# Attention scores of a 192-step macaron pipeline in two bursts, with the second half of W1's products between them

## Chip, cores and metric

One core of one Trainium2 chip. The metric is the device time of the kernel in microseconds, median of the runs.

## The reference, cut to what matters

```python
def _L0_ffn_ref(x, ...):              # called twice, with _L0_attn_ref between
    for i in range(6):
        x = attn_layer(shift_tokens(x), Wqkv[i], q_scale[i], k_scale[i], Wo[i]) + x
        x = ffn_layer(shift_tokens(x), ln_g[i], ln_b[i], W1[i], b1[i], W2[i], b2[i]) + x
    return x
# attn_layer: 16 heads of 64, q and k normalised and rotated, then in windows of 32
#   each with the window before it:
sim = einsum('bhwie,bhwje->bhwij', q, look(k)) * 8.0   # masked, softmax over 64 keys
out = einsum('bhwij,bhwje->bhwie', softmax(sim), look(v))
# ffn_layer: layer norm, then
hg = xn @ W1 + b1; a, gate = split(hg, 2)
return a * gelu(gate) @ W2 + b2       # W1 is 128 x 682, W2 is 341 x 128

x = x + 0.5 * _L0_ffn_ref(_layernorm(x), ...)
x = x + _L0_attn_ref(_layernorm(x), ...)      # a linear recurrence over time
x = x + 0.5 * _L0_ffn_ref(_layernorm(x), ...)
```

The input is 2 x 1024 tokens of 128 channels in float32.

## The kernel before, in words

The 2048 tokens are 16 tiles of 128, and the two passes through six layers are 12 layers, so there are 192 tiles of work (`T`). The kernel is a software pipeline written out by hand: in step `s` every engine works on several tiles at once, each at another lag behind `s`: the token shift and transpose at lag 0 (`L_X`), the projections of q and k at lag 1 (`L_QKV`), `values` (projection of v), the transposes of q and k, and the scores at lag 2 (`L_S`), the softmax at 3 (`L_SM`), attention times values and Wo at 4 (`L_AV`, `L_WO`), the first half of the feed-forward layer at 5 (`L_F`), its second half at 6 (`L_F2`). All 198 steps are unrolled into one long program for each engine; there are no loops left on the chip. Each engine runs its own list in order, and semaphores that count steps tie the lists together (`k.wait(sem, lag)`).

TensorE's list in a step (`step` in the tensor block): the projections `project(1)`, `project(0)` (line 484), eight transposes of q (line 495), `attend` (line 539), `project(2)`, `project(3)`, eight transposes of k (line 495), Wo (line 594), eight transposes of the probabilities (line 602), the transpose of the normed tile (line 607), W2 (line 622), `values(1)` and `values(0)` (line 490), the transpose of the next tile (line 639), `hidden(1)` and `hidden(0)`, that is the gate half and the other half of W1's products (line 503), and last `scores`.

`hidden(k, a)` writes three products of 128x114 weights into `proj[:, a, :]`, each as two passes in float32. `proj` is a PSUM tile of two banks that q, k, v and W1's products share, so `hidden(k, a)` waits for `a_v[a]`, ScalarE's copy of the v tile out of the same bank (line 677). ScalarE's gelu (line 740) reads the bank of `hidden(1)` and needs another activation table than the exponential; VectorE's `hT` (line 1001) multiplies gelu's result with the bank of `hidden(0)`, and waits for `p_f[0]` and `a_gelu`.

`scores` first writes a mask into the two banks of `sps` (line 519, one product of 128x512 in bfloat16 for each) and then adds, for each of 8 head pairs, 2 bank halves, 2 window groups and 2 heads, a small product of 64x32 weights (line 527): 64 products, each in two passes, each with its own weight load. The last one signals `p_S`, for which VectorE's maximum (line 1008) waits; ScalarE's copies into `qT` and `kT` wait for it a step later. Bank 0 of `sps` also holds the scratch values of VectorE's reciprocal root, so the scores wait for `v_rs` (its last step is `rn`, line 848), for `v_sub` (VectorE's subtraction that has read the last scores), for `a_qT`, `a_kT`, and in even steps for `a_car`. After it the next step begins with `project(1)`, which waits for `a_xT` (ScalarE's last write of `xsT`, line 750) and `a_gelu`; `project(0)` waits for `v_h` (VectorE's `hT`).

Of the kernel before, what the change touches and what calls it, by code (L numbers as in the profile page):

```python
# [25 lines left out]
PAIRS = HEADS // 2  # L26
# [20 lines left out]
L_X, L_QKV, L_S, L_SM, L_AV, L_WO, L_F, L_F2 = 0, 1, 2, 3, 4, 4, 5, 6  # L47
# [10 lines left out]
def macaron(nc, x_in, w_in, w_out, b_out, w_qkv, q_scale, k_scale, w_o,  # L58
            w_1, w_2, b_2, c_cols, c_rope, c_mask, c_ident, out):
    with ExitStack() as ctx:  # L60
# [3 lines left out]
        def sem(name):  # L64
            return ctx.enter_context(nc.semaphore(name))
# [86 lines left out]
        p_xT, p_qT, p_kT, p_S, p_pT = sem("p_xT"), sem("p_qT"), sem("p_kT"), sem("p_S"), sem("p_pT")  # L152
# [6 lines left out]
        a_v = [sem(f"a_v{c}") for c in range(2)]  # L159
# [308 lines left out]
        def _(pe):  # L468
# [29 lines left out]
            def hidden(k, a):  # L498

                at = (k.ffn if k.reg is not None else (k.s - L_F) // TILES % DEPTH) * 2 * FH  # L500
                for c in range(3):
                    rows = min(FC, FH - c * FC)
                    last = mm(proj[0:rows, a, c * P:(c + 1) * P],  # L503
                              w1[:, at + a * FH + c * FC:at + a * FH + c * FC + rows],
                              xnT[:, :], start=True, stop=True, skip_group_check=True)
                last.then_inc(p_f[a], 1)
# [4 lines left out]
                    mm(ops[:, 1, 0:3 * P], hT[:, 0, :], hT[:, :, :].rearrange("p c n -> p (c n)"), start=True, stop=True,  # L511
                       skip_group_check=True)

            def scores(k):
                first = k.off("first", L_S, lambda u: ((POS - 1 - u % POS) // (POS - 1)) * 512)
                par = k.parity(L_S)
                for ty in range(2):
                    m = mask[:, bass.ds(first, 512)] if ty == 0 else mask[:, 0:512]
                    mm(sps[:, ty, :], idb[:, :], m, start=True, stop=False, skip_group_check=True)
                for p in range(PAIRS):  # L520
                    for ty in range(2):
                        for g in range(2):
                            for hp in range(2):
                                w = 2 * ty + g
                                at, rows = par * P + w * WIN, slice(hp * DH, (hp + 1) * DH)
                                to = (2 * g + (hp ^ ty)) * WIN
                                last = mm(sps[to:to + WIN, ty, p * 64:(p + 1) * 64], qT[rows, p, w * WIN:(w + 1) * WIN],  # L527
                                          kT[rows, p, at:at + 2 * WIN], start=False, stop=True, skip_group_check=True)
                last.then_inc(p_S, 1)

            def attend(k):
                par = k.parity(L_AV)
# [11 lines left out]
            def step(k):  # L544
# [44 lines left out]
                if k.on(L_WO):  # L589
# [3 lines left out]
                    for p in range(PAIRS):  # L593
                        last = mm(ops[:, 0, 0:P], oT[:, p, :], wo[:, bass.ds(w + p * P, P)], start=(p == 0),  # L594
                                  stop=(p == PAIRS - 1))
                    last.then_inc(p_wo, 1)
                if k.on(L_SM):
# [3 lines left out]
                    for p in range(PAIRS):  # L601
                        last = tr(tps[:, p, :], prob[:, p, :, :].rearrange("p a b -> p (a b)"), idf[:, :])  # L602
# [5 lines left out]
                if k.on(L_F2):  # L608
# [12 lines left out]
                    for c in range(3):  # L621
                        last = mm(ops[:, 1, 3 * P:4 * P], hT[0:FC, c, :], w2[0:FC, bass.ds(at + c * P, P)],
                                  start=(c == 0), stop=(c == 2))
# [16 lines left out]
                if k.on(L_F):  # L640
                    k.wait(a_xnT, L_F)
                    if k.s == L_F:
                        pe.wait_ge(d_mlp, 16 * len(mlp_consts))
                    for a in (1, 0):
                        k.wait(a_v[a], L_S)
                        hidden(k, a)
                if k.on(L_S):

                    k.wait(v_sub, L_S + 1)
                    k.wait(v_rs, L_QKV, per=RS_STEPS)  # L650
                    k.wait(a_qT, L_S)
                    k.wait(a_kT, L_S)
                    if k.parity(L_S) == 0:
                        k.wait_even(a_car, L_S)
                    if k.reg is None and k.s == L_S:
                        pe.wait_ge(s_idb, 1)
                        pe.wait_ge(s_mask, 1)
                    scores(k)

            pe.wait_ge(c_zero2, 1)  # L660
            idle(WARM)
            pe.wait_ge(d_id, 16)
            pe.wait_ge(c_zero, 1)
            pipeline(pe, step)

# [563 lines left out]
```

## Time and profile before

| | us |
|---|---|
| median of 3 runs | 3307.64 (3303.78 to 3307.83) |
| the profiled execution's own time | 3302.78 |
| its span, first to last instruction | 3301.0 |
| PE busy | 3177.7 (96%) |
| PE weight loads busy | 2377.1 (72%) |
| DVE busy | 2994.8 (91%) |
| ACT busy | 2543.2 (77%) |
| POOL busy | 2229.6 (68%) |

PE is TensorE's matmuls and PEld its weight loads, which overlap them; DVE is VectorE, ACT ScalarE, POOL GpSimd. Durations of matmuls overlap, since they are pipelined: the distance from one start to the next tells what one costs. In a timeline each row is a run of equal instructions with its start, its length to the end of the last, and its count; in brackets stands how long the engine was idle before it and what ended that. "issue" is idle time for which the profile shows no wait. L503 is line 503 of the kernel.

### The profile page before, as it was taken

How to read it: one execution, taken by the hardware profiler on the slowest of the kernel's cores; microseconds unless marked ns; L12 is line 12 of the kernel's file. 1: busy time of each engine (PE TensorE's matmuls, PEld its weight loads, DVE VectorE, ACT ScalarE, POOL GpSimd, SP SyncE). 2: the span in 40 equal slices, each digit the busy share in tenths (PEclk: the TensorE clock that was granted, in tenths of full speed). 3: DMA queues.
4: the chain of work that ended last, by engine and by line, in shares of the span. 5: the costliest groups of instructions: out<-in, count | busy, mean ns of one | idle time of the engine just before them, and what ended most of it. 6: DMA issues, size and time to landing. Idle time of an engine off the chain costs nothing. (4 is left out here: it accounts for less than half of the span.)

```text
span 3301.0 us, 125954 instructions
## 1 busy us (share of the span) xinstructions
PE 3177.7 (96%) x50984; PEld 2377.1 (72%) x51176; DVE 2994.8 (91%) x7143; ACT 2543.2 (77%) x4144; POOL 2229.6 (68%) x1454
## 2 busy tenths in 40 slices
PE   7999999999999999999889999999999999999998
PEld 3777777777777777776667777777777777777776
DVE  7999999999899999999999998899999999999995
ACT  3877878777787777777667777788777777887775
POOL 6666666666666666667777766666666666666663
PEclk9999999999999999999999999999999999999999
DMA  4111111111111111111111111111111111111111
GB/s 124 44 48 44 48 45 48 45 48 44 47 45 48 45 48 45 47 44 39 37 37 47 45 48 45 40 48 46 45 44 48 45 48 45 48 45 48 47 52 38
DMA packets 134996, 155.84 MB, mean 47 GB/s; under 512 B 75539, under 2 KB 108439, under 8 KB 134423
## 3 DMA queue, kind: packets, MB, share of 16 engines
q1 hardware_dynamic: 129815, 144.42, 15.9%
q8 instruction: 413, 6.77, 0.9%
q10 hardware_dynamic: 4608, 3.34, 0.4%
q14 instruction: 160, 1.31, 0.1%
HBM read 33.38 MB, written 1.05 MB: 10 GB/s over the span
## 5 line engine op out<-in xcount | busy, mean ns | idle before, releaser
L1084 POOL TENSOR_TENSOR rot<-rot,swp 128x1024 f32<-128x1024 f32 x384 | 907.2, 2363 | 132.5 <-DVE rot L867 132.5
L484 PE MATMUL proj<-wq,xsT 128*128 128x512 f32 x1536 | 773.4, 622 | 55.9 <-DVE hT L1001 22.4
L673 ACT ACTIVATE sq<-proj 128x512 f32<-128x512 f32 x768 | 437.6, 596 | 400.6 <-PE proj L484 387.3
L1093 POOL TENSOR_TENSOR rot<-rot,rn 128x1024 f32<-128x1024 f32 x384 | 724.6, 1910 | 0.0
L1074 POOL TENSOR_TENSOR rt<-rt,half 128x1 f32<-128x1 f32 x192 | 105.8, 551 | 743.1 <-DVE rt L937 743.1
L861 DVE TENSOR_TENSOR swp<-proj,tab 128x512 f32<-128x512 f32 x768 | 522.0, 680 | 9.4 <-ACT sq L673 5.1
L867 DVE TENSOR_TENSOR rot<-proj,tab 128x512 f32<-128x512 f32 x768 | 518.9, 676 | 1.7 <-PE tps L495 1.6
L495 PEld LDWEIGHTS tps<-idf,rot 128*128 128x128 f32 x3072 | 362.6, 141 | 207.1 <-issue 205.1
L1078 POOL TENSOR_TENSOR prob<-prob,rr 128x1024 f32<-128x1024 f32 x192 | 365.8, 1905 | 174.7 <-DVE rr L949 174.7
L484 PEld LDWEIGHTS proj<-wq,xsT 128*128 128x128 f32 x1536 | 257.5, 189 | 293.0 <-issue 138.1
L495 PE MATMUL tps<-idf,rot 128*128 128x128 f32 x3072 | 402.0, 274 | 3.5 <-POOL rot L1093 1.9
L594 PE MATMUL ops<-wo,oT 128*128 128x128 f32 x3072 | 376.3, 276 | 4.0 <-ACT oT L695 4.0
L539 PE MATMUL ops<-pT,vb 128*64 128x64 f32 x6144 | 379.3, 225 | 0.0
L490 PE MATMUL proj<-wq,xsT 128*128 128x512 f32 x768 | 369.5, 601 | 3.5 <-DVE rot L867 3.3
L539 PE MATMUL ops<-pT,va 128*64 128x64 f32 x6144 | 369.6, 222 | 0.0
L594 PEld LDWEIGHTS ops<-wo,oT 128*128 128x128 f32 x3072 | 359.8, 193 | 4.3 <-issue 4.2
L527 PEld LDWEIGHTS sps<-kT,qT 64*32 64x32 f32 x24576 | 258.4, 105 | 121.5 <-issue 121.1
L722 ACT COPY pT<-tps 64x1024 f32<-64x1024 f32 x192 | 193.2, 1006 | 187.3 <-PE tps L602 187.3
L1001 DVE SCALAR_TENSOR_TENSOR hT<-proj,cols,fg 114x128 f32<-114x128 f32 (+1 forms) x576 | 166.8, 345 | 187.4 <-issue 179.1
L539 PEld LDWEIGHTS ops<-pT,vb 128*64 128x64 f32 x6144 | 311.6, 138 | 32.9 <-issue 32.6
L527 PE MATMUL sps<-kT,qT 64*32 64x64 f32 x24576 | 296.2, 225 | 33.3 <-issue 33.2
L503 PEld LDWEIGHTS proj<-xnT,w 128*114 128x114 f32 (+1 forms) x2304 | 273.5, 178 | 73.7 <-issue 67.9
(104 smaller groups left out, 6164.6 us busy)
## 6 DMA issues: line engine op xcount, KB each, us to landing
vb<-va SPq DMA_DIRECT2D x192, 384.0 KB, 3.5
vb<-va SPq DMA_DIRECT2D x192, 128.0 KB, 3.6
wq<-in_L_ffn_Wqkv SPq DMA_DIRECT2D x95, 192.0 KB, 3.4
xs<-Z SPq DMA_DIRECT2D x192, 32.0 KB
wo<-in_L_ffn_Wo SPq DMA_DIRECT2D x94, 64.0 KB, 2.8
xs<-Z SPq DMA_DIRECT2D x192, 28.0 KB
xs<-Z SPq DMA_DIRECT2D x192, 3.8 KB
xs<-Z SPq DMA_DIRECT2D x192, 0.2 KB
```

The lines of the kernel that those rows point to most:

```text
L484: mm(proj[:, c % 2, :], xsT[:, k.parity(L_QKV), 0:P], wq2[:, bass.ds(w + c * 512, 512)], start=True, stop=True).then_inc(p_qkv[c], 1)
L490: mm(proj[:, c, :], xsT[:, k.parity(L_S), 0:P], wq2[:, bass.ds(w + (4 + c) * 512, 512)], start=True, stop=True).then_inc(p_v[c], 1)
L495: last = tr(tps[:, p, :], rot[:, g * INNER + p * P:g * INNER + (p + 1) * P], idf[:, :])
L527: last = mm(sps[to:to + WIN, ty, p * 64:(p + 1) * 64], qT[rows, p, w * WIN:(w + 1) * WIN], kT[rows, p, at:at + 2 * WIN], start=False, stop ...
L539: last = mm(o4[hp * DH:(hp + 1) * DH, :, g, :], v, pT[:, 2 * p + g, hp, :, :].rearrange("p t i -> p (t i)"), start=True, stop=True, skip_g ...
L594: last = mm(ops[:, 0, 0:P], oT[:, p, :], wo[:, bass.ds(w + p * P, P)], start=(p == 0), stop=(p == PAIRS - 1))
L673: fn(sq[:, c * 512:(c + 1) * 512], proj[:, c % 2, :], ACT.Square).then_inc(a_sq[c], 1)
L861: v.tensor_tensor(halves(swp[:, c * 512:(c + 1) * 512]), swapped, tab[:, bass.ds(po + (2 * g + 1) * POS * DH, DH)] .rearrange("p (a d) -> ...
L867: v.tensor_tensor(heads(rot[:, c * 512:(c + 1) * 512]), heads(src), tab[:, bass.ds(po + 2 * g * POS * DH, DH)].unsqueeze(1) .to_broadcast( ...
L1078: g_.tensor_tensor(pr, pr, rr[:, :].unsqueeze(2).to_broadcast([P, HEADS, 2 * WIN]), ALU.mult).then_inc(g_nrm, 1)
L1084: g_.tensor_tensor(r, r, swp[:, g * INNER:(g + 1) * INNER], ALU.add).then_inc(g_add[g], 1)
L1093: g_.tensor_tensor(r, r, rn[:, g * HEADS:(g + 1) * HEADS].unsqueeze(2) .to_broadcast([P, HEADS, DH]), ALU.mult).then_inc(g_nm[g], 1)
```

## The change

The scores of a step are issued in two bursts of four head pairs instead of one burst of eight, and `hidden(0)` stands between them instead of ahead of the masks. The masks, with the waits of the scores, follow `hidden(1)`. `p_S` is signalled by the last product of the second burst.

```diff
--- before.py
+++ after.py
@@ -511,13 +511,15 @@
                     mm(ops[:, 1, 0:3 * P], hT[:, 0, :], hT[:, :, :].rearrange("p c n -> p (c n)"), start=True, stop=True,
                        skip_group_check=True)
 
-            def scores(k):
+            def masks(k):
                 first = k.off("first", L_S, lambda u: ((POS - 1 - u % POS) // (POS - 1)) * 512)
-                par = k.parity(L_S)
                 for ty in range(2):
                     m = mask[:, bass.ds(first, 512)] if ty == 0 else mask[:, 0:512]
                     mm(sps[:, ty, :], idb[:, :], m, start=True, stop=False, skip_group_check=True)
-                for p in range(PAIRS):
+
+            def scores(k, pairs):
+                par = k.parity(L_S)
+                for p in pairs:
                     for ty in range(2):
                         for g in range(2):
                             for hp in range(2):
@@ -526,7 +528,7 @@
                                 to = (2 * g + (hp ^ ty)) * WIN
                                 last = mm(sps[to:to + WIN, ty, p * 64:(p + 1) * 64], qT[rows, p, w * WIN:(w + 1) * WIN],
                                           kT[rows, p, at:at + 2 * WIN], start=False, stop=True, skip_group_check=True)
-                last.then_inc(p_S, 1)
+                return last
 
             def attend(k):
                 par = k.parity(L_AV)
@@ -641,9 +643,8 @@
                     k.wait(a_xnT, L_F)
                     if k.s == L_F:
                         pe.wait_ge(d_mlp, 16 * len(mlp_consts))
-                    for a in (1, 0):
-                        k.wait(a_v[a], L_S)
-                        hidden(k, a)
+                    k.wait(a_v[1], L_S)
+                    hidden(k, 1)
                 if k.on(L_S):
 
                     k.wait(v_sub, L_S + 1)
@@ -655,7 +656,13 @@
                     if k.reg is None and k.s == L_S:
                         pe.wait_ge(s_idb, 1)
                         pe.wait_ge(s_mask, 1)
-                    scores(k)
+                    masks(k)
+                    scores(k, range(PAIRS // 2))
+                if k.on(L_F):
+                    k.wait(a_v[0], L_S)
+                    hidden(k, 0)
+                if k.on(L_S):
+                    scores(k, range(PAIRS // 2, PAIRS)).then_inc(p_S, 1)
 
             pe.wait_ge(c_zero2, 1)
             idle(WARM)
```

## Rows read from the trace of the kernel before

**Rows 1.** The page: span, and busy time of each engine, share, instructions.
```profile
span 3301.0 us, 125954 instructions
...
PE 3177.7 (96%) x50984; PEld 2377.1 (72%) x51176; DVE 2994.8 (91%) x7143; ACT 2543.2 (77%) x4144; POOL 2229.6 (68%) x1454
```

**Rows 2.** The view of cores: span and mean granted TensorE clock.
```profile
core 0: 3301.0 us, clock 0.994
```

**Rows 3.** Timeline of PE: mask products of five following steps (start, us, engine, line).
```profile
293.65 0.38 PE L519 MATMUL sps<-mask,idb 128*128 128x512 bf16 x1
...
310.09 0.38 PE L519 MATMUL sps<-mask,idb 128*128 128x512 bf16 x1
...
327.41 0.38 PE L519 MATMUL sps<-mask,idb 128*128 128x512 bf16 x1
...
343.85 0.38 PE L519 MATMUL sps<-mask,idb 128*128 128x512 bf16 x1
...
360.21 0.38 PE L519 MATMUL sps<-mask,idb 128*128 128x512 bf16 x1
```

**Rows 4.** Timeline of PE, 824.05 to 828.5 us: the end of one step.
```profile
824.08 1.64 PE L503 MATMUL proj<-xnT,w 128*114 128x128 f32 x12
825.77 0.38 PE L519 MATMUL sps<-mask,idb 128*128 128x512 bf16 x1
826.08 1.48 PE L527 MATMUL sps<-kT,qT 64*32 64x64 f32 x128
827.68 1.10 PE L484 MATMUL proj<-wq,xsT 128*128 128x512 f32 x2
```

**Rows 5.** Line 527, the score passes: ns of one, least, median, most.
```profile
L527 PE MATMUL sps<-kT,qT x24576: 212/216/241, 40.1 to 3267.2; 64*32 64x64 f32 x200
```

**Rows 6.** Timeline of PE, 427.5 to 430 us: behind a late burst.
```profile
428.38 0.33 PE L527 MATMUL sps<-kT,qT 64*32 64x64 f32 x12 [0.87 <-issue]
428.66 1.54 PE L484 MATMUL proj<-wq,xsT 128*128 128x512 f32 x3
```

**Rows 7.** Timelines of ACT and of DVE, 824 to 829 us, same step.
```profile
824.17 0.59 ACT L677 COPY va<-proj 128x512 f32<-128x512 f32 x1 [0.23 <-PE proj L490]
824.78 1.28 ACT L740 ACT_TABLE_LOAD   x1
826.07 0.89 ACT L740 ACTIVATE fg<-proj,cols 114x128 f32<-114x128 f32 x3
...
827.38 0.20 ACT L750 ACTIVATE xsT<-xsT 64x1 f32<-64x1 f32 x1
...
824.56 0.19 DVE L848 SCALAR_TENSOR_TENSOR rn<-rt,sps 128x32 f32<-128x32 f32 x1
...
827.41 0.87 DVE L1001 SCALAR_TENSOR_TENSOR hT<-proj,cols,fg 114x128 f32<-114x128 f32 x3 [1.40 <-issue]
828.19 1.21 DVE L1008 TENSOR_REDUCE mx<-sps 128x16 f32<-128x1024 f32 x1
```

**Rows 8.** Timeline: `values` in the same step, its load and its four passes.
```profile
823.01 0.30 PEld L490 LDWEIGHTS proj<-wq,xsT 128*128 128x128 f32 x2 [0.60 <-DVE rot L867]
...
822.21 1.92 PE L490 MATMUL proj<-wq,xsT 128*128 128x512 f32 x4
```

**Rows 9.** Timeline of PEld: three bursts that stop; idle before in brackets.
```profile
310.40 1.24 PEld L527 LDWEIGHTS sps<-kT,qT 64*32 64x32 f32 x118 [0.42 <-issue]
312.69 0.17 PEld L527 LDWEIGHTS sps<-kT,qT 64*32 64x32 f32 x10 [1.06 <-issue]
...
426.13 1.22 PEld L527 LDWEIGHTS sps<-kT,qT 64*32 64x32 f32 x116 [0.42 <-issue]
428.38 0.17 PEld L527 LDWEIGHTS sps<-kT,qT 64*32 64x32 f32 x12 [1.03 <-issue]
...
194.02 1.24 PEld L527 LDWEIGHTS sps<-kT,qT 64*32 64x32 f32 x119 [0.42 <-issue]
196.86 0.16 PEld L527 LDWEIGHTS sps<-kT,qT 64*32 64x32 f32 x9 [1.60 <-issue]
```

**Rows 10.** The page, part 3: packets, MB, share of 16 DMA engines.
```profile
q8 instruction: 413, 6.77, 0.9%
```

**Rows 11.** Waits view: us in total, times, longest.
```profile
PEld sps L527 <- issue: 121.1, 232, 1.7
```

**Rows 12.** Windows view, line 527's loads from the burst's start: us, busy (x).
```profile
826.08:826.69 0.61, 0.61 (x67) 1.00 0.03 0
826.08:827.37 1.29, 1.29 (x128) 1.00 0.01 0
```

**Rows 13.** Timeline of PE: into and out of `attend`, and four passes unhindered.
```profile
813.10 1.04 PE L495 MATMUL tps<-idf,rot 128*128 128x128 f32 x8
814.07 0.28 PE L539 MATMUL ops<-pT,vb 128*64 128x64 f32 x2
...
815.86 0.29 PE L539 MATMUL ops<-pT,va 128*64 128x64 f32 x4
816.08 1.98 PE L484 MATMUL proj<-wq,xsT 128*128 128x512 f32 x4
...
805.89 1.88 PE L490 MATMUL proj<-wq,xsT 128*128 128x512 f32 x4
```

**Rows 14.** Timeline of PEld about the middle, 1620 to 1640 us.
```profile
1632.49 0.30 PEld L484 LDWEIGHTS proj<-wq,xsT 128*128 128x128 f32 x2 [2.34 <-DVE hT L1001]
```

## Prediction

> **What bounds the kernel now.** I read the busy shares first, then the timeline of the end of one step, then the waits of TensorE's weight loads, because the change only reorders TensorE's program. TensorE is busy 96% of the span, VectorE 91% [rows 1], and the granted clock is full nearly throughout [rows 2], so the clock has no part in this. The kernel is 192 pipelined steps, and the mask products of following steps start 16.44, 17.32, 16.44 and 16.36 us apart [rows 3]. Two questions follow: what sets the 16.4, and what makes one step 0.9 longer.
>
> What sets 16.4: at the end of a step (window 824 to 829) TensorE runs W1's twelve passes (`hidden`), the masks and the burst of 128 score passes, then the next step's first projection [rows 4]. The last score pass starts at 826.08 + 1.48 - 0.22 = 827.34 [rows 4, 5], the projection at 827.68, that is 0.34 later. After a burst that ended late for another reason the same hand-over took 428.66 - (428.38 + 0.33 - 0.22) = 0.17 [rows 6]. So TensorE waits some 0.15 here, and for this: ScalarE copies the value tile out at 824.17, loads the gelu table, runs gelu and writes `xsT` until 827.38 + 0.20 = 827.58 [rows 7], and the projection's weight load starts at 827.65. The end of a step is bound by ScalarE's chain behind `values`, with TensorE 0.15 behind it. VectorE stands close too: `hT` starts after gelu, `mx` starts when `hT` is done [rows 7], and VectorE's last rotation releases the load for `values` at 823.01 [rows 8].
>
> What makes a step long: in the step of 310.40 the burst's loads run to number 118, stop for 1.06 us with nothing to wait for, and end with ten more; at 426.13 they stop after 116 for 1.03, at 194.02 after 119 for 1.60 [rows 9]. The three are 116 us, or seven steps, apart. Instructions come to TensorE over a queue of 413 packets [rows 10]; 102,160 matmuls and loads [rows 1] are 247 to a packet (with the semaphore instructions a little more) and 532 to a step. So each step uses two packets and some 0.15 of a third, and a packet's end moves through the step and is back after seven. It hurts only late in the burst, where 256 instructions are used up in 1.3 us: the next packet is usable 2.29, 2.25 and 2.84 us after the burst began [rows 9]. The waits view has 232 idle stretches before these loads, 121.1 us in all [rows 11]; 192 are the ordinary 0.42 ahead of each burst (81 us), which leaves 40 of 1.01 us. One such stall of 1.06 made its step 0.92 longer [rows 3], the rest went into the 0.15 above. Now lost: 40 x (1.01 - 0.14) = 35 us.
>
> The Trainium skill, page "Advanced Engine Details and Errata", section ISA Cache, says that an instruction cache line is 16 KB or 256 instructions and that there are two; the trace agrees in the 247 and in the seven steps.
>
> **The change, part by part.** Nothing is added or removed: the six passes of the second half of W1 with their six loads, and the wait for `a_v[0]`, move from ahead of the masks to the middle of the burst. TensorE issues no DMA. What TensorE's order costs in an ordinary step:
> - Two bursts for one. Of the present one 67 loads are under way by 0.61 us, and all 128 take 1.29 [rows 12]: the front goes faster than the rest. Two of 0.61: -0.05.
> - Into the small tiles once more. The present kernel does that ahead of `attend`: eight transposes from 813.10, beat (1.04 - 0.27) / 7 = 0.11, so that the next would start at 813.98; it starts at 814.07 [rows 13]. +0.09.
> - Out of them once more. `attend`'s last four start at 815.86 and run 0.29, so the last starts at about 815.93; the projection starts 0.15 later and its four passes take 1.98 where they take 1.88 with the load hidden [rows 13]. With the ordinary beat of 0.02 taken off: +0.24.
> - `hidden(0)` no longer waits for the copy of `va`. Its six and `hidden(1)`'s six passes take 1.64 [rows 4] where twelve at the beat of 0.11 take 11 x 0.11 + 0.27 = 1.47; half of the difference is `hidden(1)`'s own wait, which stays. -0.08.
> - The masks come up 0.75 sooner and meet their wait for `v_rs`: VectorE's `rn` ends at 824.56 + 0.19 = 824.75 [rows 7], `hidden(1)` at about 824.80. Nothing, or a mask load that isn't prefetched, 0.10. Taken: +0.05. Queued behind that wait are only the masks and scores.
> - Slack taken up: -0.15 at the projection (above), -0.04 at `values`, whose four passes take 1.92 against 1.88 [rows 8, 13] because VectorE releases them late.
>
> Sum +0.06 us. Bounds: 0 (the switches cost half, as the queue is full behind the moved passes) to +0.20 (no slack used and an unhidden mask load). The switches are the largest term: the Trainium skill, page "TensorEngine Tiling (Array Packing)", Key Properties, says that changing the tiling mode drains the engine, which speaks against the change; the trace shows it as the 0.09 and 0.24 above.
>
> Who waits for the moved work: VectorE's `hT` needs `hidden(0)`. That would now be issued 0.31 + 0.61 + 0.8 after the first mask, last pass near 826.8, seen near 827.1; gelu ends at 826.96 and `hT` mostly starts right after. It costs VectorE 0 to 0.1, inside the bounds. The scores are complete about 0.25 later than now; `mx` has that to spare while `hT` runs (0.87). ScalarE's gelu needs `hidden(1)` alone, which doesn't move. This counts in some 170 steps; for 20 about the middle (1460 to 1800 us) VectorE is the bound: TensorE's load waits 2.34 us for `hT` there [rows 14]. 170 x 0.06 = +10 us.
>
> **The stalls.** A packet that ends in the second burst now takes in `hidden(0)`: from the first score pass to the last is 0.61 + 0.24 + 0.65 + 0.09 + 0.61 = 2.2 us, against 1.27. If the next packet is usable 2.27 us after the burst's begin as now, hardly a stall is left. But no row shows when it is asked for. TensorE's instructions ahead of the present burst are held last by the wait for `a_v[0]`, 1.27 us before the burst; afterwards by the wait for `v_rs`, 0.6 before it. An order placed as soon as that wait is over comes 0.65 later, and the stall is then 2.27 + 0.65 - 2.2 = 0.7. Taken: 0.65, since two of the three stalls end 2.29 and 2.25 us after the burst's begin. It strikes when the packet's end falls on the last 34 of the 256 places (the second burst's last 30 and the projection's first 4; a place further ahead has `hidden(1)` in its packet and time enough): 192 x 34/256 = 25 steps, 16 us. Bounds: 3 us left to 30 us left. Saved: 35 - 16 = 19 us (5 to 32).
>
> **Sum.** +10 - 19 = -9 us. The profiled execution took 3302.78 us, 3301.0 of it span, so 3294 for it; it stands 4.9 below the median of 3307.64, which gives 3299.
>
> **The rivals.**
> - *The stalls go almost wholly.* The order for the packet moves with the burst, 2.2 us suffice: saved 32, cost 10 or less, -22 to -35, so 3273 to 3286. For it: 2.25 and 2.29 are nearly 2.2. Against: 2.84 at 194 us, and the later wait. 0.22.
> - *The switches win: slower.* Place: the hand-overs score, W1, score in each ordinary step. Price: 0.33 for both, and if ScalarE's `xsT` or VectorE moves along with TensorE's delay (through `hidden(0)` to `hT` to the projection's `v_h`), the 0.19 of slack isn't there: +0.17 to +0.2 a step, 30 us, less 19: +11, 3319. It decides from +0.11 a step on (170 x 0.11 = 19). For it: `hT` and `mx` sit right behind each other. Against: 0.15 of idle at the projection in most steps. 0.20.
> - *The stalls only change place.* An order 0.65 later and a slower transfer leave 1 us each time on 25 to 30 steps; saved 8, cost 10: 3309, no change. 0.16.
> - My forecast: 0.42, its own range 3292 to 3306.
>
> That the change doesn't do what it says I leave out: the diff has every product once and the same waits.
>
> **How the numbers follow.** About 0.2% (6.6 us) is what a measurement of this kernel can tell from no change; the forecast of -9 lies just past it, so of its 0.42 I give 0.27 to faster and 0.15 to the same. Faster 0.27 + 0.22 = 0.49, same 0.15 + 0.16 = 0.31, slower 0.20. The range takes in the stall-free rival and the slower one: 3276 to 3324, about a tenth beyond either end.
>
> **What would show it.** Idle stretches before score loads of near 1 us: from 40 to some 25 of 0.65, all near the end of the second burst or at the projection behind it. The ordinary step from 16.40 to about 16.46. The projection's load no longer 0.24 late behind `xsT`. `hT` at most 0.1 later against gelu. The forecast is wrong if the ordinary step is 16.52 or more (then slower), or if stalls at scores are gone (then 3280). In the middle 20 steps nothing should move.

## The result, and the profile after

| | before | after |
|---|---|---|
| median of 5 runs each | 3307.64 us (3300.16 to 3307.96) | 3319.07 us (3316.81 to 3320.97) |
| span of the profiled execution | 3301.0 | 3316.7 |
| ordinary step (mean of two neighbours) | 16.40 | 16.52 |

The ratio is 1.0041, with a 95% interval of 1.0028 to 1.0053: the change makes the kernel slower by 0.4%. The page, the view of cores and two rows of the waits view after:

```profile
span 3316.7 us, 126146 instructions
...
PE 3229.7 (97%) x51176; PEld 2389.1 (72%) x51176; DVE 2997.6 (90%) x7143; ACT 2543.1 (77%) x4144; POOL 2229.9 (67%) x1454
...
q8 instruction: 413, 6.77, 0.8%
```
```profile
core 0: 3316.7 us, clock 0.995
```
```profile
PEld sps L529 <- issue: 115.1, 237, 1.7
PEld proj L484 <- DVE hT L1008: 37.0, 23, 2.9
```

VectorE, ScalarE, GpSimd, the clock and the instruction packets stand as before [rows 1, 2, 10]. PE's busy time is 52 us up, but that is mostly no work: before, the first of the two mask products has no record in any step [rows 3, x1], and now it has (x2, 0.59 us where 0.38 stood), which alone is 192 x 0.21 = 40 us. The idle time before score loads was 121.1 us in 232 stretches [rows 11]; it is 115.1 in 237. With 192 ordinary stretches of 0.42 taken off, 40 stalls of 1.01 us have become 45 of 0.77, 34.5 us in all. So the stalls, which the forecast wanted to see shrink to 16 us, shrank by 6, twice the 3 us by which two executions of one kernel differ (numbers 5 and 6 below).

The end of an ordinary step, of PE, PEld, ACT and DVE:

```profile
843.25 0.82 PE L503 MATMUL proj<-xnT,w 128*114 128x128 f32 x6
844.02 0.59 PE L518 MATMUL sps<-mask,idb 128*128 128x512 bf16 x2
844.54 0.86 PE L529 MATMUL sps<-kT,qT 64*32 64x64 f32 x64
845.33 0.91 PE L503 MATMUL proj<-xnT,w 128*114 128x128 f32 x6
846.17 0.86 PE L529 MATMUL sps<-kT,qT 64*32 64x64 f32 x64
846.96 1.55 PE L484 MATMUL proj<-wq,xsT 128*128 128x512 f32 x3
...
846.96 0.30 PEld L484 LDWEIGHTS proj<-wq,xsT 128*128 128x128 f32 x2
...
845.24 0.88 ACT L747 ACTIVATE fg<-proj,cols 114x128 f32<-114x128 f32 x3
846.55 0.20 ACT L757 ACTIVATE xsT<-xsT 64x1 f32<-64x1 f32 x1
...
843.74 0.19 DVE L855 SCALAR_TENSOR_TENSOR rn<-rt,sps 128x32 f32<-128x32 f32 x1
846.28 0.87 DVE L1008 SCALAR_TENSOR_TENSOR hT<-proj,cols,fg 114x128 f32<-114x128 f32 x3 [1.10 <-PE proj L503]
847.07 1.23 DVE L1015 TENSOR_REDUCE mx<-sps 128x16 f32<-128x1024 f32 x1
```

`xsT` is complete at 846.75, the projection's load starts at 846.96, 0.21 later; before it was 0.07 later [rows 7: 827.58, 827.65]. ScalarE no longer sets the end of the step. TensorE does: its last score pass starts at 846.17 + 0.86 - 0.22 = 846.81 and the projection 0.15 behind it, which is what a hand-over takes without any wait (0.17 in [rows 6]). `hT` and `mx` are in place as before, so VectorE isn't the new bound either.

Where the 15.7 us of span come from: I took the distance between the transposes of the normed tile in following steps. In the two stretches of 80 steps on either side of the middle, the steps without a stall became 16.414 to 16.543 and 16.442 to 16.557 long, that is +0.12 x 160 = +19.5 us. What the stalled steps last beyond that fell from 32.3 us (31 steps) to 30.8 (40 steps). Both stretches together, whichever steps are called stalled: 2659.9 to 2677.7, +17.8. The 23 steps in the middle took 426.8 and take 425.9; start and end give the remaining -1.2.

Timeline of PE, the mask products of four following steps, the third of which holds a stalled burst; then timeline of PEld, that burst and two later ones:

```profile
394.19 0.59 PE L518 MATMUL sps<-mask,idb 128*128 128x512 bf16 x2
...
410.76 0.59 PE L518 MATMUL sps<-mask,idb 128*128 128x512 bf16 x2
...
427.23 0.59 PE L518 MATMUL sps<-mask,idb 128*128 128x512 bf16 x2
...
444.38 0.59 PE L518 MATMUL sps<-mask,idb 128*128 128x512 bf16 x2
```
```profile
427.75 0.70 PEld L529 LDWEIGHTS sps<-kT,qT 64*32 64x32 f32 x64 [0.42 <-issue]
...
429.38 0.60 PEld L529 LDWEIGHTS sps<-kT,qT 64*32 64x32 f32 x52
430.48 0.17 PEld L529 LDWEIGHTS sps<-kT,qT 64*32 64x32 f32 x12 [0.50 <-issue]
...
1112.22 0.70 PEld L529 LDWEIGHTS sps<-kT,qT 64*32 64x32 f32 x64 [0.42 <-issue]
...
1114.85 0.13 PEld L529 LDWEIGHTS sps<-kT,qT 64*32 64x32 f32 x2 [0.32 <-issue]
...
1129.12 0.70 PEld L529 LDWEIGHTS sps<-kT,qT 64*32 64x32 f32 x64 [0.42 <-issue]
...
1130.75 0.51 PEld L529 LDWEIGHTS sps<-kT,qT 64*32 64x32 f32 x43
1131.86 0.26 PEld L529 LDWEIGHTS sps<-kT,qT 64*32 64x32 f32 x21 [0.59 <-issue]
```

Steps of 16.57, 16.47 and, with the stall, 17.15. The stall is seen in the load that follows it: the next packet is usable 430.48 - 427.75 = 2.73, 2.63 and 2.74 us after the first burst's begin, where it was 2.25 to 2.29 in two of the three bursts of [rows 9]. These three are at the low end. In the whole trace score loads start more than 0.2 us late 48 times after and 40 times before; these stalls end 2.01 to 3.30 us after the begin, median 2.81, where they ended after 1.20 to 2.86, median 2.25. And a stall hits two steps in a row: at 1114.85 with 2 loads left, at 1131.86 with 21 left, at nearly the same time after the begin. The 48 stalls come behind load 84 to load 127 of the step's 128 (before: 86 to 127), so a packet's end further ahead in that stretch gets no earlier packet.

### The profile page after: what moved, and what is told of

Its sections match the earlier page's. It is cut to its first block and busy times, and to the rows that moved or that the text cites. A ratio compares the mean times of both kernels' runs of the same rounds, so it can differ in the third digit from the quotient of the medians.

```text
span 3316.7 us, 126146 instructions
## 1 busy us (share of the span) xinstructions
PE 3229.7 (97%) x51176; PEld 2389.1 (72%) x51176; DVE 2997.6 (90%) x7143; ACT 2543.1 (77%) x4144; POOL 2229.9 (67%) x1454
## 5 line engine op out<-in xcount | busy, mean ns | idle before, releaser
L529 PEld LDWEIGHTS sps<-kT,qT 64*32 64x32 f32 x24576 | 270.3, 105 | 140.2 <-issue 115.1
L529 PE MATMUL sps<-kT,qT 64*32 64x64 f32 x24576 | 339.6, 224 | 26.5 <-issue 26.5
L1008 DVE SCALAR_TENSOR_TENSOR hT<-proj,cols,fg 114x128 f32<-114x128 f32 (+1 forms) x576 | 166.7, 345 | 203.6 <-PE proj L503 202.1
L503 PE MATMUL proj<-xnT,w 128*114 128x128 f32 (+1 forms) x2304 | 343.0, 285 | 1.3 <-ACT xnT L734 0.7
```

The source lines that it names most:

```text
L503: last = mm(proj[0:rows, a, c * P:(c + 1) * P], w1[:, at + a * FH + c * FC:at + a * FH + c * FC + rows], xnT[:, :], start=True, stop=True, ...
```

## The experiments

The ratios are to the kernel before on the same chip, with 95% intervals. The theory after the result had two parts. **S**: two bursts cost an ordinary step 0.25 to 0.3 of TensorE's time, of which 0.15 is slack. **A**: the packet is asked for only when the last wait ahead of the burst is over, and the new order has a later one (`v_rs`). The rivals were that the moved `hidden(0)` does the harm through `hT` (**V**), and that the packet's time has to do with the burst's length and not with a wait (**B**). The edits of numbers 1, 3, 4, 8, 10 and 11 are shown against the changed kernel, those of 2, 7, 9 and 12 against the kernel before. "By the single loads" means that I counted each stop of some 0.4 us or more between two score loads that follow each other.

**1. Masks and W1 in the new order, scores in one burst.**

```diff
                     masks(k)
-                    scores(k, range(PAIRS // 2))
                 if k.on(L_F):
                     k.wait(a_v[0], L_S)
                     hidden(k, 0)
                 if k.on(L_S):
-                    scores(k, range(PAIRS // 2, PAIRS)).then_inc(p_S, 1)
+                    scores(k, range(PAIRS)).then_inc(p_S, 1)
```

> Masks behind hidden(1), hidden(0) behind the masks, then one burst of eight pairs: the first half of the change without the split. Theory A (what costs is going out of the small tiles and back in, and a second tail of a burst): no further change of tiles here, so the ordinary step stays at 16.40 us, with TensorE waiting a little longer than 0.15 us for xsT at its end; some 40 stalls of about 1 us in the burst stay; ratio to before 0.998 to 1.001. Theory B (the earlier wait of the masks for v_rs costs): ordinary step 16.45 or more. Theory C (the next instruction packet is asked for once the last held wait ahead of the burst is over, and that is now v_rs, as far ahead of the burst as a_v[0] was): the stalls end 2.25 us after the burst's begin, as before.

Measured: 3308.44 against 3308.24, ratio 0.9999 (0.9987 to 1.001). The ordinary step is 16.40 again. A row of its waits view and its timeline of PE:

```profile
PEld sps L529 <- issue: 55.9, 52, 1.7
```
```profile
591.30 0.59 PE L518 MATMUL sps<-mask,idb 128*128 128x512 bf16 x2
591.73 0.82 PE L503 MATMUL proj<-xnT,w 128*114 128x128 f32 x6
592.47 1.49 PE L529 MATMUL sps<-kT,qT 64*32 64x64 f32 x128
594.12 1.10 PE L484 MATMUL proj<-wq,xsT 128*128 128x512 f32 x2 [0.16 <-ACT xsT L756]
```

Here the load ahead of a burst no longer stands idle 0.42, so nearly all of the 52 stretches are stalls: 48 of 1.13 us by the single loads. The projection waits 0.16 for `xsT`, the slack made visible. The stalls end 2.29 us after the begin in the median, with the last wait (`v_rs`, `a_v[0]`) 1.3 us ahead of it as before. Moving the masks ahead of `hidden(0)`, with `v_rs` behind `hidden(1)`, costs nothing in time; what costs lies in the second burst. The 48 stalls are some twelve more than the kernel before has by the same count (33 and 36, number 5). Why, and why the time doesn't show them, is open.

**2. The kernel before, with one of W1's products made twice.** It measures the slack.

```diff
+                if a == 0:
+                    last = mm(proj[0:rows, a, c * P:(c + 1) * P],
+                              w1[:, at + a * FH + c * FC:at + a * FH + c * FC + rows],
+                              xnT[:, :], start=True, stop=True, skip_group_check=True)
                 last.then_inc(p_f[a], 1)
```

> The kernel before with the last product of W1's second half made twice: two more passes of 0.11 us on TensorE at the end of a step and nothing else. Theory A (TensorE has 0.15 us of slack against ScalarE's xsT there, and is the bound beyond it): ordinary step 16.40 + 0.22 - 0.15 = 16.47, about +12 us in all. Rival (no slack, TensorE is the bound already): 16.62, +37 us. Rival (TensorE is not the bound, VectorE is): 16.40 and no change.

Measured: 3314.69, ratio 1.0018 (1.0006 to 1.003). Two passes more at the beat of 0.11, or 0.22, made the ordinary step 0.05 longer (16.45): the slack is 0.17, against 0.15 in the prediction.

**3. Two bursts with nothing of W1 between them, only each half's masks.**

```diff
-                    k.wait(a_v[1], L_S)
-                    hidden(k, 1)
+                    for a in (1, 0):
+                        k.wait(a_v[a], L_S)
+                        hidden(k, a)
...
-                    masks(k)
+                    masks(k, 0)
                     scores(k, range(PAIRS // 2))
-                if k.on(L_F):
-                    k.wait(a_v[0], L_S)
-                    hidden(k, 0)
-                if k.on(L_S):
+                    masks(k, 1)
                     scores(k, range(PAIRS // 2, PAIRS)).then_inc(p_S, 1)
```

> W1's products where they stood before, both halves ahead of the masks; the masks are written in two halves of 256 columns, one pair ahead of each burst of four head pairs. The same change of tiles as in the changed kernel with W1 not moved. Theory A: +0.33 for the two switches, +0.04 for the second tail, -0.15 of slack: ordinary step 16.60, about +35 us less what the stalls give. Rival (moving W1's half to where VectorE needs it late is what costs): 16.40.

Measured: 3326.59, ratio 1.0063 (1.0042 to 1.0084). Its PE, ordinary step, and PEld of a stalled one:

```profile
631.14 0.86 PE L530 MATMUL sps<-kT,qT 64*32 64x64 f32 x64
631.93 0.39 PE L518 MATMUL sps<-mask,idb 128*128 128x256 bf16 x2
632.25 0.86 PE L530 MATMUL sps<-kT,qT 64*32 64x64 f32 x64
```
```profile
597.02 0.70 PEld L530 LDWEIGHTS sps<-kT,qT 64*32 64x32 f32 x64 [0.21 <-issue]
...
598.14 0.61 PEld L530 LDWEIGHTS sps<-kT,qT 64*32 64x32 f32 x55 [0.21 <-issue]
599.77 0.16 PEld L530 LDWEIGHTS sps<-kT,qT 64*32 64x32 f32 x9 [1.02 <-issue]
```

From one burst's last pass to the next one's first it is 632.25 - (631.14 + 0.64) = 0.47, of which two mask products of half the width take 0.21: the two switches cost 0.26 here. The ordinary step is 16.51, +0.11, with `hidden(0)` where it was and `hT` as before. That speaks against V: the cut itself costs the step its length. With only 0.47 between the bursts the stalls are 36 of 1.09 us by the single loads. In the stall shown the packet is usable 2.75 us after the begin (2.73 in the median of the stalls over 0.4 us); I had not seen that in this order, too, the last wait stands nearer to the first burst, 1.11 us ahead of it where it was 1.32. That is 0.2 nearer for a median 0.46 later than the 2.27 of the kernel before, more than the wait explains; but the median itself moves by some 0.2 between runs whose wait stands in one place (2.50 in number 9).

**4. Seven head pairs, `hidden(0)`, one head pair.**

```diff
-                    scores(k, range(PAIRS // 2))
+                    scores(k, range(7))
...
-                    scores(k, range(PAIRS // 2, PAIRS)).then_inc(p_S, 1)
+                    scores(k, range(7, PAIRS)).then_inc(p_S, 1)
```

> The changed kernel with seven pairs in the first burst and one in the second. Theory A with VectorE behind it: the same switches, but hidden(0) is 0.5 us later, so that hT starts some 0.5 later than in the changed kernel and VectorE becomes the bound: ordinary step 16.9 or more. If VectorE has the room: 16.52 as in the changed kernel. Stalls (arrival of the packet at about 2.7 us after the first score pass): those that fall before product 112 no longer have hidden(0) ahead of them and last about 1.7 us; if instead W1's products themselves delay the request, they get shorter.

Measured: 3420.27, ratio 1.0343 (1.0314 to 1.0373), far above what either theory said. The DVE timeline and a row of the waits view:

```profile
590.18 0.87 DVE L1008 SCALAR_TENSOR_TENSOR hT<-proj,cols,fg 114x128 f32<-114x128 f32 x3 [1.63 <-PE proj L503]
590.97 1.21 DVE L1015 TENSOR_REDUCE mx<-sps 128x16 f32<-128x1024 f32 x1
```
```profile
DVE hT L1008 <- PE proj L503: 326.8, 174, 4.5
```

VectorE now waits for `hidden(0)` in almost every step (202.1 us in 170 stretches in the changed kernel, most of it before it would have started anyway), and the step, as the mean of two neighbours, is 16.97. V is a real mechanism, which the cut at four pairs escapes: there `hT` comes 0.05 later in the step, here 0.85. The stalls ahead of the 112th product last 1.4 us and not the 1.7 expected; since the bound has changed too, I take nothing from them.

**5 and 6. Both kernels once more**, unedited, for the spread between executions.

> The kernel before once more, for a second profile: how far the stalls of one execution stand for all. Ordinary step 16.40 us; idle stretches before the score loads other than the ordinary ones: between 33 and 50 of about 1 us, ending about 2.25 us after the first score pass.

> The changed kernel once more, for a second profile. Ordinary step 16.52 us; some 45 stalls of 0.77 us, ending about 2.7 us after the first score pass.

Measured: spans 3306.9 and 3318.9; 36 stalls of 1.15 us and 42 of 0.85 by the single loads (in the first profiles 33 of 1.15 and 43 of 0.77). The ordinary steps are 16.40 and 16.52 again. The step is steady to 0.01; the sum of the stalls moves by some 3 us from one execution to the next.

**7 and 8. The scratch values of VectorE's reciprocal root in SBUF, so that the scores need no `v_rs`**, in either kernel. It was to take away the late wait.

```diff
+        scr = sb("scr", [3 * 2 * HEADS])
...
-                    k.wait(v_rs, L_QKV, per=RS_STEPS)
...
-            xsq, rsq, usq = [sps[:, 0, 2 * HEADS * n:2 * HEADS * (n + 1)] for n in range(3)]
+            xsq, rsq, usq = [scr[:, 2 * HEADS * n:2 * HEADS * (n + 1)] for n in range(3)]
```

> The kernel before with the reciprocal root's scratch values in SBUF and no wait of TensorE for v_rs: the control for the next run. In the order of before that wait is over before the one for a_v[0], so nothing should change: ratio 0.998 to 1.002, ordinary step 16.40. If VectorE's small operations cost more or less from SBUF, this run shows it.

> The changed kernel with the same scratch in SBUF and no wait for v_rs. Theory A (the next instruction packet arrives a fixed 3.4 us after the last wait that holds TensorE's instructions ahead of the burst; that wait is v_rs in the changed kernel, 0.6 to 0.75 us ahead of the first score pass, and is now a_v[1], 1.25 ahead): stalls end 2.2 us after the first score pass instead of 2.7, so that nearly none is left; ordinary step 16.52 stays; total about 3290, ratio 0.993 to 0.997, faster than both. Rival B (the arrival is fixed by the burst's begin or by the transfer, not by the wait): stalls stay at 45 of 0.77 us, total 3317.

Measured: 3689.32, ratio 1.1161 (1.1142 to 1.118), and 3682.18, ratio 1.1137 (1.112 to 1.1153). The experiment was spoilt by something else: groups of lines of number 7, and after them of the kernel before:

```profile
L828 DVE TENSOR_TENSOR ru<-rt,scr 128x32 f32<-128x32 f32 x192 | 433.6, 2258 | 0.1
L816 DVE TENSOR_SCALAR scr<-scr 128x32 f32<-128x32 f32 x192 | 190.8, 994 | 0.0
```
```profile
L828 DVE TENSOR_TENSOR ru<-rt,sps 128x32 f32<-128x32 f32 x192 | 34.7, 180 | 0.1
L816 DVE TENSOR_SCALAR sps<-sps 128x32 f32<-128x32 f32 x192 | 36.4, 190 | 0.0
```

The same small operations last 2258 ns for 180 and 994 for 190, once all their operands lie in SBUF; the step is 18.5 us. The stalls can still be read. With one burst there are 42 of 1.21 us, with two bursts ten, 6.6 us in all by the waits view and five of them over 0.4 us, in the same slow step and without the late wait. That is for A, but in a kernel with another bound and more time ahead of every burst.

**9 and 10. The root's last correction left out**, in either kernel, so that `v_rs` comes 0.44 us earlier. What these two compute lacks that correction.

```diff
-        RS_STEPS = 12
+        RS_STEPS = 10
...
-                elif n == 10:
...
-                elif n == 11:
...
-                    for n in (8, 10, 11, 12):
+                    for n in (8, 12):
```

> The kernel before with two of the ten steps of VectorE's reciprocal root left out (the last correction; q and k are then scaled otherwise), so that v_rs comes some 0.45 us earlier and VectorE has 0.4 us less to do a step: the control for the next run. In this order the last wait that holds TensorE's instructions ahead of the burst is the one for a_v[0]. Both theories: ordinary step 16.40 (it is bound by TensorE's and ScalarE's chain), 35 to 50 stalls of about 1.1 us that end 2.25 us after the first score pass. In the middle, where VectorE is the bound, some 8 us are saved.

> The changed kernel with the same two steps left out. Theory A (a held wait for v_rs ahead of the burst delays the request for the next instruction packet): v_rs now comes 0.45 us sooner, so stalls end about 2.3 us after the first score pass instead of 2.7, at the very end of the second burst: at most some 10 of more than 0.4 us are left, ordinary step 16.52; 20 to 28 us faster than the changed kernel beyond what the middle saves. Rival B (the arrival hangs on the burst, not on the wait): 45 stalls of 0.8 us as in the changed kernel.

Measured: 3300.86, ratio 0.9986 (0.9974 to 0.9997), and 3300.68, ratio 0.998 (0.9969 to 0.9992). Rows of the waits view of 9 and of 10, and a burst of 10 that stalls:

```profile
PEld sps L527 <- issue: 120.1, 231, 1.9
```
```profile
PEld sps L529 <- issue: 100.4, 228, 2.0
```
```profile
426.08 0.70 PEld L529 LDWEIGHTS sps<-kT,qT 64*32 64x32 f32 x64 [0.42 <-issue]
...
427.71 0.60 PEld L529 LDWEIGHTS sps<-kT,qT 64*32 64x32 f32 x52
428.71 0.17 PEld L529 LDWEIGHTS sps<-kT,qT 64*32 64x32 f32 x12 [0.40 <-issue]
```

This is the pair that tells A from B. Before, the shorter root moves nothing in the stalls: 39 of 1.01 us by the waits view, and what stalled steps cost in the two stretches is 33.3 us against 32.3. In the changed kernel it takes them from 45 of 0.77 to 36 of 0.55, and what they cost from 30.8 us in 40 steps to 14.3 in 25. The two stretches as a whole go from 2659.9 to 2659.7 us in the kernel before and from 2677.7 to 2660.5 in the changed one. The stalls over 0.2 us now end 2.23 to 3.31 us after the begin, median 2.61 where it was 2.81; a packet that is usable before the burst gets to its place leaves no trace here, so the true shift is larger, how much is not shown. The transfer that ends those over 0.4 us starts 1.2 us after `rn` ends and 0.7 after the copy of `va`, where both were 1.0 to 1.1 in the changed kernel: it has moved with `v_rs` and not with `a_v[0]`. The ordinary steps stay 16.40 and 16.52. So what the stalls cost is 33.3 with one burst and 14.3 with two, the saving of 19 us that I had predicted, once the wait is early, and the switches cost the 19 us back: both kernels then take the same.

**11. The cut by PSUM bank** (`masks` and `scores` take the banks to be written, and all eight pairs of one bank follow each other): bank 1's mask and scores, `hidden(0)`, then the wait for `v_rs`, bank 0's mask and scores. The wait sits in the middle, where `hidden(0)` covers it.

```diff
-                    k.wait(v_rs, L_QKV, per=RS_STEPS)
...
-                    masks(k)
-                    scores(k, range(PAIRS // 2))
+                    masks(k, (1,))
+                    scores(k, (1,))
...
-                    scores(k, range(PAIRS // 2, PAIRS)).then_inc(p_S, 1)
+                    k.wait(v_rs, L_QKV, per=RS_STEPS)
+                    masks(k, (0,))
+                    scores(k, (0,)).then_inc(p_S, 1)
```

> Two bursts by bank instead of by head pair: hidden(1), the mask and all scores of bank 1, hidden(0), then the wait for v_rs, the mask and all scores of bank 0, which alone holds the root's scratch. The same work and the same two extra changes of tiles. Theory A: nothing slow is waited for ahead of the first burst but a_v[1], the packet arrives 2.2 us or less after its begin, the two bursts last 2.5: the stalls are nearly gone; ordinary step 16.52 or a little more; total about 3290, ratio 0.993 to 0.997, faster than both kernels. Rival B: stalls as in the changed kernel, 3317.

Measured: 3363.34, ratio 1.0175 (1.016 to 1.0191), a miss. The timeline of PEld:

```profile
588.37 0.94 PEld L529 LDWEIGHTS sps<-kT,qT 64*32 64x32 f32 x64 [0.32 <-issue]
...
590.45 0.94 PEld L529 LDWEIGHTS sps<-kT,qT 64*32 64x32 f32 x64 [0.32 <-issue]
```

Eleven short stops are left, 3.7 us in all. That doesn't tell A from B: from the first pass to the last it is 2.97 us here, long enough for most packets that come after 2.8 as well.
**12. One burst, bank 1's scores ahead of bank 0's**, to price that order by itself.

```diff
-                    scores(k)
+                    masks(k, (1, 0))
+                    scores(k, (1, 0)).then_inc(p_S, 1)
```

> The control for the run by bank: W1's products and the waits as in the kernel before, one burst, but the scores of bank 1 ahead of those of bank 0. If the order of the banks has no price of its own: 16.40 and 3305 to 3309, ratio 0.999 to 1.001. If products that follow each other in one bank are slower, the burst's 1.27 us grow, and the first 0.15 of that is free.

Measured: 3335.84, ratio 1.009 (1.0073 to 1.0107). One row of its PEld:

```profile
586.92 1.73 PEld L529 LDWEIGHTS sps<-kT,qT 64*32 64x32 f32 x128 [0.42 <-issue]
```

The 128 loads take 1.73 for 1.29 [rows 12], and the ordinary step is 16.64: +0.24 for +0.44, the slack being used. The order by bank has its own price, which explains number 11's miss.

None of the twelve beats both kernels with the whole computation in it. What would follow from them, the root's scratch in another PSUM bank, wasn't tried: all banks are in use.

## Why the prediction was wrong

The direction was wrong: -9 us was said, +11 to +14 came. Two sums failed: the stalls, where 19 us were to be saved and some 2 were, and the ordinary step, where +10 us was said and +19.5 came.

- **What bounds the kernel**: right. The end of the step is ScalarE's chain with TensorE 0.15 behind it; number 1 shows the wait (0.16), number 2 measures 0.17 by another way.
- **The switches**: right. From the 64th pass to the 65th I had reckoned 0.24 + 0.65 + 0.09, about 1.0; it is 846.17 - (844.54 + 0.86 - 0.22) = 0.99. Number 3 has 0.26 for the pair of switches, with bfloat16 masks between, where I had 0.33.
- **Two bursts for one, -0.05**: wrong by 0.07. I read 67 loads in 0.61 us [rows 12] as the pace of a short burst. A burst of 64 takes 0.64 to its last pass, twice 1.285, one of 128 takes 1.267: +0.02. The fast first half is there in the short burst too, but so is the pause of 0.08 behind load 32 and a slower second half.
- **`hidden(0)` without its wait, -0.08, and the masks' wait for `v_rs`, +0.05**: together -0.08 instead of -0.03 (number 1, which has this move alone, shows 0.05 to 0.08). The masks follow `hidden(1)` without a gap (844.02, 0.77 behind 843.25). With the 0.33 and the 0.02 that makes 0.27 for the last score pass, where the terms had given 0.25: errors that nearly cancel.
- **Slack, -0.15 and -0.04**: the first was taken up in full, 0.27 - 0.15 = 0.12. The second wasn't: `values` comes 0.78 us and `hidden(1)` 2.65 us behind the transpose of the normed tile in both kernels. That VectorE's rotation, which it waits for, moves along with the projections that feed it would explain this; no run tests it. So the ordinary step is +0.12, not +0.06, the bound of "16.52 or more" that the prediction named for being wrong. The mechanism was right and the sum 0.06 short: 0.07 for the two bursts and 0.04 for the slack at `values`, less the 0.05 of the masks.
- **The stalls, 25 of 0.65, 19 us saved**: the step that failed. The length was nearly right (0.77). The number was 34 places of 256; 45 of 192 steps are 60 places. I let a packet whose end lies ahead of the last 15 loads have "time enough", but 26 of the 48 stalls over 0.2 us come ahead of load 113. The wait for `v_rs` stands ahead of both bursts, and what is asked for behind it comes some 2.8 us after the first burst's begin (median; the three shown 2.63 to 2.74), 0.56 later than before, whether the packet ends behind load 107 or 126 (1131.86 and 1114.85). So the late wait, which I had counted as a delay for a few places, gave back nearly all that the longer burst had won. Numbers 9 and 10 show this cause: the same wait 0.44 earlier, and 16.5 us come back in the changed kernel, none in the one before.
- **What a stall costs**: right. I took 0.14 of slack off each stall before and none after, 35 us lost before; stalled steps cost 32.3. With the slack gone, the 6 us by which the stalls shrank are only 1.5 us of steps, which can't be told from nothing with the spread of 3 us between executions.
- **The rivals**: "the switches win" gave 3319 and has the measured time, by other terms than its own: a step of +0.12 for its +0.17 to +0.2, with the slack there that it had denied, and 2 us saved for its 19. Its condition, decided from +0.11 a step on, held by 0.01, but hung on that 19; with what was saved, +0.01 would have been enough. "The stalls only change place" described the stalls best (shifted later, nearly as costly) and had the step too cheap.
- **Small points**: `hT` moved 0.05 (0 to 0.1 was said), the middle -0.9 us (nothing was said), the projection's load no longer waits for `xsT` (said).

The Trainium skill, page "TensorEngine Tiling (Array Packing)", section Key Properties, says that a change of the tiling mode drains the engine. The trace agrees, with 0.33 us for a pair of switches around W1's products and 0.26 around masks, against 0.17 us of slack.

## What to carry to other kernels

To cut a dense burst of small matmuls is to buy two switches of the array's mode, here some 0.3 us, each time; it pays only where the engine has that much slack in every step, or where what goes away costs more than that in the mean over all steps (here 40 stalls in 192 steps, 0.18 us a step). A stall for instructions is not set by the burst alone: look at the last wait ahead of it. Here the next packet was usable 3.5 to 3.9 us after that wait, by the medians of the kernels' stalls over 0.4 us, and a change that moves a wait closer to the burst takes back what it gives. Price a short burst by a short burst, not by the front of a long one.

## What the runs showed of the chip that I had not expected

- **Instruction packets**: in the trace's records of the instruction queue, the transfer that ends a stall of over 0.4 us starts 1.0 to 1.3 us after the last wait ahead of the burst, by the medians of the kernels (before: the copy of `va`, 1.3 us ahead of the burst, transfer 0.1 ahead of it; after: `rn`, 0.6 ahead, transfer 0.4 behind), and the packet is usable 2.4 to 2.6 us after the transfer's start. In 11 of the 40 stalls before, the transfer starts already 0.8 to 1.1 us ahead of the burst, which is as long behind the earlier copy of `va`, the one that `hidden(1)` waits for (2.1 ahead); these stalls end after 1.2 to 1.8 us. After the change none starts that early.
- **The burst**: the loads come every 6 to 7 ns up to the 32nd, then there is a pause of 0.08 us and one of 0.06, then they come every 8 to 9 ns. With four tiles in turn instead of eight, every fourth load 36 ns (64 loads in 0.94 for 0.70 us).
- **VectorE beside GpSimd**: 180 ns became 2258 and 190 became 994, when operands moved from PSUM to SBUF while GpSimd was at work; in number 7 one such operation starts at 504.78 and lasts until GpSimd's operation on `rot`, 504.64 with 2.35 us, is over. The Trainium skill, page "SBUF — State Buffer", section "SBUF: two separate sides", says that the two engines share a pair of ports which one of them holds for a whole instruction. The trace agrees, with these numbers. Scratch values in PSUM keep small operations out of it.
